# Values of a 16-head block attention: one projection for four tiles, repeated by DMA, masked on POOL

## What is computed

```python
qkv = (xn @ Wqkv.T).reshape(B, L, 3, H, HD).transpose(2, 0, 3, 1, 4)   # H = 16, HD = 8
q, k, v = qkv[0], qkv[1], qkv[2];  q, k = _rope(q), _rope(k)
att = einsum('bhnqd,bhnkd->bhnqk', qb, kb) * scale                     # n: blocks of 32 tokens
att = softmax(where(causal, att, min))
s = einsum('bhnqk,bhnkd->bhnqd', att, vb).reshape(B, L, D) @ Wout.T
```

## Time and profile before

| | |
|---|---|
| median of 3 runs | 910.92 us (910.48 to 911.56) |
| the profiled execution | 909.12 us, its span 907.3 us |
| PE, PEld busy | 803.8 us (89%), 616.1 us (68%) |
| DVE busy | 677.0 us (75%) |
| ACT busy | 645.5 us (71%) |
| POOL busy | 531.6 us (59%) |
| DMA packets | 64704, 48.24 MB |

### The profile page before, as it was taken

The page is one execution under the profiler, slowest core; times in us unless marked ns, Lnnn a source line. Parts: engine busy times, 40 slices in busy tenths (PEclk is TensorE's granted clock), DMA queues, the critical chain, the costliest instruction groups (busy, mean ns, idle before and its releaser), DMA issues.

```text
span 907.3 us, 26209 instructions
## 1 busy us (share of the span) xinstructions
PE 803.8 (89%) x9912; PEld 616.1 (68%) x9912; DVE 677.0 (75%) x1389; ACT 645.5 (71%) x2037; POOL 531.6 (59%) x529
## 2 busy tenths in 40 slices
PE   4979999779999999999889887999999999988985
PEld 3558777557777777778766555777877777775652
DVE  4788898777887887787466767778787788746765
ACT  1217677579989899889743237988988998964463
POOL 1494233178888888888610008888888888951100
PEclk9999999989999999999999999999999999999998
DMA  7220001012222222222201122222222222222001
GB/s 272 73 52 4 3 4 41 3 48 54 51 64 57 60 51 63 53 63 54 60 19 24 23 52 54 63 55 57 58 61 56 62 51 61 57 51 100 0 35 58
DMA packets 64704, 48.24 MB, mean 53 GB/s; under 512 B 40410, under 2 KB 50948, under 8 KB 64068
## 3 DMA queue, kind: packets, MB, share of 16 engines
q1 hardware_dynamic: 64580, 46.57, 19.9%
HBM read 10.63 MB, written 2.10 MB: 14 GB/s over the span
## 4 chain that ended last, share of the span: by engine, by line
PE 55%; DVE 17%; ACT 17%; issue 7%; POOL 2%; DMA 1%; SPq 0%; DVEq 0%; POOLq 0%; ACTq 0%
PE ps L404 46%; PE ps L414 9%; ACT prob L862 6%; DVE nmax L1124 3%; ACT sq L804 3%; DVE nt L1152 2%; ACT V L831 2%; ACT oT L813 2%; DVE split L952 2%; ACT kT L838 1%; ACT pT L808 1%; DVE prob L1211 1%; DVE split L950 1%; ACT qT L823 1%; DVE vexp L1043 1%
## 5 line engine op out<-in xcount | busy, mean ns | idle before, releaser
L862 ACT ACTIVATE prob<-ps,nmax 128x128 f32<-128x128 f32 x512 | 181.8, 375 | 35.6 <-DVE nmax L1124 35.5
L404 PE MATMUL ps<-wqkv,split 128*128 128x512 f32 x576 | 186.8, 435 | 13.4 <-DVE split L952 9.9
L1349 POOL TENSOR_TENSOR prob<-prob,rinv 128x512 f32<-128x512 f32 x128 | 133.7, 1045 | 87.2 <-DVE rinv L1110 45.8
L404 PEld LDWEIGHTS ps<-wqkv,split 128*128 128x128 f32 x576 | 96.9, 194 | 32.5 <-DVE split L952 10.0
L1124 DVE TENSOR_REDUCE nmax<-ps 128x4 f32<-128x512 f32 x128 | 83.6, 686 | 47.0 <-PE ps L404 47.0
L414 PE MATMUL ps<-ident,prob 128*128 128x128 f32 x640 | 97.8, 276 | 14.1 <-POOL prob L1349 13.2
L862 ACT ACTIVATION_READ_ACCUMULATOR prob<-ps,nmax 128x1 f32 x512 | 109.2, 213 | 0.0
L1360 POOL TENSOR_TENSOR qr<-qr,ss 128x512 f32<-128x512 f32 x64 | 66.9, 1045 | 52.1 <-DVE qr L1136 52.1
L414 PEld LDWEIGHTS ps<-ident,prob 128*128 128x128 f32 x640 | 75.6, 141 | 28.3 <-POOL prob L1349 17.5
L404 PE MATMUL ps<-oT,wo 128*128 128x128 f32 x512 | 73.9, 287 | 22.2 <-ACT oT L813 22.2
L404 PEld LDWEIGHTS ps<-oT,wo 128*128 128x128 f32 x512 | 62.1, 191 | 37.5 <-ACT oT L813 36.5
(11 more groups left out here) (134 smaller groups left out, 1886.3 us busy)
## 6 DMA issues: line engine op xcount, KB each, us to landing
VB<-V SPq DMA_DIRECT2D x129, 128.0 KB, 2.4
kT<-kT SPq DMA_DIRECT2D x65, 128.0 KB, 2.4
XS<-X SPq DMA_DIRECT2D x32, 128.0 KB, 2.3
XS<-X SPq DMA_DIRECT2D x128, 32.0 KB, 1.9
D<-in_xT SPq DMA_DIRECT2D x8, 256.0 KB, 4.9
XS<-in_xT SPq DMA_DIRECT2D x2, 1024.0 KB, 6.3
out_T<-XS SPq DMA_DIRECT2D x8, 256.0 KB, 2.0
raw<-in_wqkv SPq DMA_DIRECT2D x2, 768.0 KB, 3.9
```

Of the source, the lines that this page charges most:

```text
L404: return nc.tensor.matmul(o, l, r, start=start, stop=stop, skip_group_check=True)
L862: nc.scalar.activation(prob[:, par, grp, s * P:(s + 1) * P], ps[:, 4 + grp, s * P:(s + 1) * P], ACT.Exp, bias=nmax[:, par, grp * 4 + s:grp ...
L1349: g.tensor_tensor(p4, p4, rinv[:, slot, 4 * grp:4 * grp + 4].unsqueeze(2).broadcast_to([P, 4, P]), ALU.mult).then_inc(l_prob, 1)
```

## The change

The values are computed from `X` itself, in its natural order, for one chunk (four tiles) at a time: four products in bank 4, one copy on ACT into `vt` (memory of `oT`, two buffers). SyncE then issues 16 DMAs for the chunk, one for each partition group r and block b; each copies [32 partitions, 4 tiles, 128 values] (64 KB, runs of 512 bytes) to group r. So every partition group holds the values of every block. There are two destinations: a new tile `vrep_own` for even chunks and `arot` for odd ones. POOL multiplies with `pmask` from there, behind `kexp` of the same tile. The queries are read from `qA` in place, and ACT's copies for `qst` and `xst` are gone. The values of chunk c+1 are computed in step 4c, on TensorE before `awo`, on ACT at the end of the step. Those of chunk 0 are computed before the last `a_project`.

```diff
-        qst, xst = kT[:, :, 0, 0:P], qT
+        vrep_own = sb("vrep_own", [P, 2 * SEQ])
+        vt = oT
-        oAT = sb("oAT", [P, 2, P])
+        oAT = VB[:, 1, 0:2 * P].rearrange("p (s t) -> p s t", s=2)
+        def copies(c):
+            return (arot[:].rearrange("p i t -> p (i t)") if c % 2 else vrep_own[:]).rearrange("p (k v) -> p k v", k=TPC)
```

SyncE, behind the eight `copy_shifted` calls:

```diff
+            for c in range(CHUNKS):
+                sp.wait_ge(a_vt, c + 1)
+                if c == 1:
+                    sp.wait_ge(a_tab, 4 * CHUNKS)
+                elif c > 1:
+                    sp.wait_ge(a_vexp, TPC * (c - 1))
+                src = vt[:, c % 2, :].rearrange("p (k v) -> p k v", k=TPC)
+                for r in range(INGRP):
+                    for b in range(BLKS):
+                        sp.dma_start(copies(c)[32 * r:32 * r + 32, :, b * P:(b + 1) * P],
+                                     src[32 * b:32 * b + 32, :, :]).then_inc(v_rep, 16)
```

TensorE:

```diff
+            def a_values(c):
+                pe.wait_ge(x_new, max(c + 1, CHUNKS - 1))
+                wait(pe, a_vt, c)
+                for k in range(TPC):
+                    last = mm(ps[:, 4, k * P:(k + 1) * P], part(X, c * TPC + k, P), awv[:])
+                last.then_inc(a_v, 1)
-            steps(-2, CHUNKS - 1, a_project)
+            steps(-2, CHUNKS - 2, a_project)
+            a_values(0)
+            a_project(CHUNKS - 1, 1)
...
-                    pe.wait_ge(a_stat, n + 2)
+                    pe.wait_ge(a_rot, 2 * CHUNKS)
-                                      qst[32 * g:32 * g + 32, nxt, 32 * b:32 * b + 32],
+                                      qA[32 * g:32 * g + 32, (n + 1) * P + 32 * b:(n + 1) * P + 32 * b + 32],
...
-                if live(n, 1, TILES):
-                    wait(pe, a_vexp, n + 1)
-                    for b in range(BLKS):
-                        last = mm(ps[:, 4, P * b:P * b + P], xst[:, nxt, b, :], awv[:])
-                    last.then_inc(a_v, 1)
+                if n % TPC == 0 and live(n, TPC, TILES):
+                    a_values(n // TPC + 1)
```

ScalarE, ahead of `a_tile` (with a call for chunk 0) and in it:

```diff
+            def a_values(c):
+                act.wait_ge(a_v, c + 1)
+                wait(act, v_rep, 16 * INGRP * BLKS * (c - 1))
+                nc.scalar.activation(vt[:, c % 2, :], ps[:, 4, :], ACT.Copy).then_inc(a_vt, 1)
...
-                if live(n, 2, TILES):
...
-                    nc.scalar.activation(qst[:, par, :], part(qA, n + 2, P), ACT.Copy)
-                    nc.scalar.activation(xst[:, par].rearrange("p b (r t) -> p b r t", r=INGRP),
-                                         part(X, n + 2, P).rearrange("p (b t) -> p b t", b=BLKS).unsqueeze(2)
-                                         .broadcast_to([P, BLKS, INGRP, ABLK]), ACT.Copy).then_inc(a_stat, 1)
...
+                if n % TPC == 0 and live(n, TPC, TILES):
+                    a_values(n // TPC + 1)
```

VectorE loses its product with `pmask`:

```diff
-                    dve.wait_ge(a_v, n + 2)
-                    wait(dve, a_o, n)
-                    v.tensor_tensor(vexp[:, nxt, :].rearrange("p (b h c) -> p b h c", h=INGRP, c=VW)[:, :, :, 0:AHD],
-                                    ps[:, 4, :].rearrange("p (b h c) -> p b h c", h=INGRP, c=AHD),
-                                    pmask[:].unsqueeze(1).unsqueeze(3).broadcast_to([P, BLKS * GROUPS, INGRP, AHD]),
-                                    ALU.mult).then_inc(a_vexp, 1)
```

GpSimd, in `a_tile` behind `kexp`:

```diff
+                    pool.wait_ge(v_rep, 16 * INGRP * BLKS * (n // TPC + 1))
+                    wait(pool, a_o, n - 1)
+                    g.tensor_tensor(vexp[:, par, :].rearrange("p (b h c) -> p b h c", h=INGRP, c=VW)[:, :, :, 0:AHD],
+                                    copies(n // TPC)[:, n % TPC, :].rearrange("p (b h c) -> p b h c", h=INGRP, c=AHD),
+                                    pmask[:].unsqueeze(1).unsqueeze(3).broadcast_to([P, BLKS * GROUPS, INGRP, AHD]),
+                                    ALU.mult).then_inc(a_vexp, 1)
```

More of the change, by code:

```diff
@@ L206, in build @@
         a_rot = sem("a_rot")
-        a_stat = sem("a_stat")
+        a_vt = sem("a_vt")
+        v_rep = sem("v_rep")
         a_kexp = sem("a_kexp")
@@ L763, in _ @@
             steps(3, CHUNKS - 1, a_project)
+            def a_values(c):
+                act.wait_ge(a_v, c + 1)
+                wait(act, v_rep, 16 * INGRP * BLKS * (c - 1))
+                nc.scalar.activation(vt[:, c % 2, :], ps[:, 4, :], ACT.Copy).then_inc(a_vt, 1)
+            a_values(0)
             def a_tile(n, par):
                 nxt = 1 - par
-                if live(n, 2, TILES):
-                    wait(act, a_score, n + 1)
-                    wait(act, a_v, n + 1)
-                    nc.scalar.activation(qst[:, par, :], part(qA, n + 2, P), ACT.Copy)
-                    nc.scalar.activation(xst[:, par].rearrange("p b (r t) -> p b r t", r=INGRP),
-                                         part(X, n + 2, P).rearrange("p (b t) -> p b t", b=BLKS).unsqueeze(2)
-                                         .broadcast_to([P, BLKS, INGRP, ABLK]), ACT.Copy).then_inc(a_stat, 1)
                 if live(n, -1, TILES):
@@ L790, in a_tile @@
                     nc.scalar.activation(part(A_OUT, n - 1, P), ps[:, 7, 0:P], ACT.Copy).then_inc(a_done, 1)
-            act.wait_ge(a_rot, 2 * CHUNKS)
-            steps(-2, TILES - 1, a_tile)
+                if n % TPC == 0 and live(n, TPC, TILES):
+                    a_values(n // TPC + 1)
+            steps(-1, TILES - 1, a_tile)
             for L in range(DEPTH):
```

## The result

The kernel after takes 970.73 us in the median (969.14 to 971.91, 4 runs) against 910.7 (909.64 to 911.56, 4 runs) before: 1.066 times as long, 95% interval 1.0636 to 1.0681, 60 us more. The forecast was 962 us with a range of 936 to 981. The result lies in that range, but 1.7 us above the 953 to 969 of the likeliest case, in what the prediction had given to the nearer half of its rival of dear copies. The profiled execution took 969.61, its span is 967.8.

The account below looks back on a forecast made before the run. TensorE was taken to bound the kernel before, the copy loop the changed one: 2.3 + 5.0 + 0.1 + 11.9 = 19.3 us; seven loops +44.1, start +6.8, giving 960.0 profiled, 962 us median, range 936 to 981.

Parts of the forecast that it names:

- likeliest case: Copies issue about 0.64 us apart on SyncE's queue and set the period: 953 to 969 us, chance 0.68.
- rival of dear copies: SyncE's queue: an issue takes 0.8 us, each copying 2.4 us longer, 981 us; at 1.0, 1005 us; chance 0.13.
- Removed work: TensorE's value products gone: plain step 2.66 us for 2.99, but this saving is hidden in the longer period.
- landed to step 4c: POOL makes vexp and then kexp between the copies' landing and TensorE's step 4c: about 2.3 us.
- step 4c to the end of ACT's copy: From TensorE's start of step 4c until ACT has copied the next chunk's values: 5.0 us at low clock.
- clock step: TensorE's idle gap before step 4c brings the lower clock, so ACT's copy ends after 5.0 us instead of 3.8.
- The copying: SyncE's 16 issues for a chunk plus one landing: 15 x 0.64 + 2.3 = 11.9 us, range 9.0 to 12.5.
- The inserts: DVE's work for the next stage behind steps 6, 12, 18 and 22, costing 7.3 us before, is hidden in the periods.
- The loop: Closed loop of four attention steps through POOL, TensorE, ACT and SyncE: 19.3 us against 13.0, +44.1 over seven.
- The start: Attention step 0 waits for chunk 0's values and copies, starting at 77.4 us instead of 70.59: 6.8 us later.
- After step 28: No more copies awaited; a low-clock start (about +0.7) against three shorter steps: nothing, within 1 us.
- rival of hidden copies: The 16 transfers run side by side with cheap issues, TensorE sets the period: -10.7 us, 900 us, chance 0.03.

Follow-up runs that it names:

- run 6: The changed kernel with nine TensorE products without use filling the idle gap ahead of each step 4c: 967.03 us, ratio 1.063.
- run 9: run 8 with chunk 1's values made in the projections, and two products without use instead of three, also ahead of step -1: 910.8 us.
- run 1: The changed kernel with POOL's kexp(n+1) ahead of vexp(n) and one semaphore for each copy buffer: 932.8 us, ratio 1.0248.
- run 2: The changed kernel with 4 of a chunk's 16 copies, the other groups reading stale values: 908.76 us, ratio 1.0001.
- run 7: run 1 with values made earlier: chunk 0 behind the third projection, chunk 1 in step -1, chunk c+1 in step 4c-2: 910.36 us.
- run 8: run 7 with three TensorE products without use added at the steps 8, 14, 20 and 24: 912.79 us, ratio 1.0034.
- run 11: run 9 with 5 DMAs through HBM instead of 16 for a chunk: 919.34 us, ratio 1.0103.
- run 12: run 2 with DVE's four inserts cut into 12 pieces, one behind each of the steps 6 to 17: 899.03 us, ratio 0.988.
- run 3: The changed kernel with all 16 copies of a chunk, each of one tile of the four (16 KB for 64 KB): 966.4 us, ratio 1.0632.
- run 5: The kernel before with queries read from qA in place, without ACT's copy into qst: 908.21 us, ratio 0.9987.
- run 10: The changed kernel with 5 DMAs for a chunk, one write to HBM and four reads back, instead of 16: 950.79 us, ratio 1.0455.

## Why the prediction held, step by step

- **Removed work.** Right: a plain step is 2.63 for the 2.66 predicted, ended by the copy of `pT`. None of it shows in the total, since the periods are set by the copies.
- **vexp on POOL** 1.04 (1.02), **landed to step 4c** 97.48 - 95.34 = 2.14 (2.3), **step 4c to the end of ACT's copy** 4.74 (5.0; the copy ends at 102.22), **SyncE** 0.03 (0.1). All right. The clock step was right in its place and size: run 6 gives back 1.1 us of a period, for the 1.2 predicted.
- **The copying** is the term that was mis-sized: from the first issue at 82.14 to `vexp` at 95.34 it is 13.2 us, where 11.9 was predicted, and above the high bound of 12.5. The median issue, 0.60, and the landing, 2.1, are no longer than assumed. But in each group of 16 one or two issues take 0.98 to 1.71 us, 13 of the 128, so that a group is 10.7 to 12.3 long instead of 16 x 0.64 = 10.2. Above 0.60 these 13 make 10.0 us, 1.25 for a group, against the 1.3 that the term lacks. No row of before had 16 in succession, as the rival of dear copies said; the result has about half of the 2.4 us that this rival added at 0.8 for an issue.
- **Where the long issues lie.** The trace has 16 KB packets of a queue that the page calls "q8 instruction", the loading of program code by its name. In the changed kernel each of the 13 long issues starts within 0.4 us of such a packet, and no such packet that starts within a group is without one; in run 9 it is 15 of 15, and a sixteenth packet, at 119.92, starts with the pause at 119.90. (In runs 1, 2, 7 and 8 one or two packets within the groups have no long issue.) The first row below is the long issue at 88.94, the second the queue from 88.7 to 90.7 in the same trace, the third the queue in the stage before, 70.6 to 161.6:

```profile
88.94 1.64 SPq L362 DMA_DIRECT2D arot<-oT  x1
...
q8 instruction: 1, 0.02, 4.4%
...
q8 instruction: 18, 0.29, 1.4%
```

  The kernel before loads 18 times in 91 us of the stage, one in 5 us, although SyncE issues next to nothing there. So the loads don't come from the copies; a series of issues meets them. That the load is what delays the issue was not tested by a run.
- **The inserts** are hidden, as predicted: in the chunk with the one at 148.39 TensorE waits 3.01 us for DVE and then 2.30 instead of 6.9 to 8.7 for the copies, and the period is 20.0.
- **The loop** is 20.2 for 19.3, so +50.7 for +44.1. That is the period, and with it the time, of the prediction's own upper bound (20.2 and 969), but not by its terms: it had 1.28 for `vexp` and 12.5 for the copying, measured are 1.04 and 13.2. **The start**, +6.9, for +6.8.
- **After step 28** "nothing, within 1 us" was wrong: +2.9, which is over the 2 us that the prediction named as the sign of a cause it doesn't have. The first products with `wqkv` ran at the lower level:

```profile
219.13 0.59 PE L422 MATMUL ps<-amask,ident_bf 128*128 128x128 bf16 x4 [7.89 <-issue]
...
230.34 2.90 PE L422 MATMUL ps<-wqkv,split 128*128 128x512 f32 x6 [1.86 <-DVE split L972]
```

  The same six took 1.64 before. That is 1.3 of the 2.9. TensorE had been idle 1.86 us ahead of them before as well; why the clock was lower this time, and the rest of the 2.9, was not traced. (Runs 8, 9 and 11 have the 2.90 too, runs 7 and 12 about the 1.64 of before.)
- **The causes.** That the waits stood in the wrong place is shown: run 1 takes away `kexp` behind the wait (-38), run 7 the missing lookahead (-22 more, with the earlier first copies), and with them the loss is gone. That the issues cost and not the bytes is shown by runs 2 and 3. The edit at q is worth nothing (run 5); ACT's copy of the tokens, `xst`, was not left out alone.
- **The rival of hidden copies** needs copying below 6.6 us to break even, by the prediction. With four issues it is about 3 x 0.64 + 2.1 = 4.0 us, and run 2 is only even. Its arithmetic of -10.7 us counted 0.6 saved at each of DVE's inserts, where POOL's second product makes the inserts longer and costs the clock. With these in pieces, run 12 measures 899.03, but that this meets the rival's 900 is in part luck: its 28 steps are 8.9 us shorter than before (82.07 for 90.97) where the rival had 11.6, and another 1.8 us lie behind step 28 (743.90 for 745.74), where it had none. So the rival's mechanism exists, for four issues and not for 16; its price is not shown. Its rule from the Trainium skill (DMA: Bandwidth & Descriptors, section on issuing engines), that starting a DMA usually takes little beside the DMA itself, does not carry over to here: an issue took 0.60 us beside a landing of 2.1, and the queue was occupied for some 11.5 of each 20.2 us. (The page gives the fit that the prediction drew on for DMAs that GpSimd issues; these are SyncE's.)

No complete kernel that was run beats the kernel before clear of noise. DVE's pieces in a complete kernel were not tried; with 16 issues the 12.6 us of run 9 would bound it.

## What to carry to other kernels

Count the DMAs between a producer and its consumer as a serial term, issues by their time on the queue plus one landing, and make the data at least one such period ahead; bytes may be a small part of it. On an engine that works in order, put a wait for a transfer behind whatever the critical engine needs next: here that alone was worth 38 of 60 us. When work moves to an idle engine, look for the instructions of another engine that used to run beside its idleness, and cut inserts on the critical chain into pieces shorter than the slack of a step.

## What was not expected of the hardware

- Issues in succession are not even: 13 of 128 take 0.98 to 1.71 us where the median is 0.60, with 64 KB and with 16 KB (13 of 128 above 0.9) alike, and the long ones lie where a load of program code starts.
- TensorE's granted clock went to 0.50 behind an idle 2.98 us and stayed there for three steps of 3.8 to 5.2 us although TensorE was busy 11.81 of 13.00 us (run 2, 117 to 130). The length of the gap doesn't decide alone: in run 2 an idle 1.68 ahead of 152.26 left it at 1.00; in the kernel before an idle 1.25 ahead of 95.62 took it down, and the same 1.25 ahead of 116.61 didn't; in run 12, with no gap above 0.61 from 81.29 to 158.56, the same stream kept 1.00.
- DVE's product of two SBUF inputs and POOL's product slow each other: 3.64 us for 1.43, and 1.49 for 1.04.
- Reading 256 KB back from HBM in runs of 512 bytes landed 5.2 to 5.4 us after the issue in the median (runs 11 and 10), against 2.1 for 64 KB within SBUF.
